# One projection per tensor with its three bf16 parts split off in PSUM, and row scatters spread two per slot over the attention slots

## The reference

```python
x = L0_attn_x                                   # (8, 512, 128)
xn = _layernorm(x, axis=-1)
x = x + attn(xn, w_attn, w_proj, decay_raw) + ffn(xn, W1, W2, Wr)

# attn: 16 heads of 8 channels, causal, with a decay over the distance
q, k, v = split(xn @ w_attn)
scores = einsum('bhqd,bhkd->bhqk', q, k) / sqrt(8) + causal + logw   # logw = -log1p(decay * log1p(dist))
y = einsum('bhqk,bhkd->bhqd', softmax(scores), v) @ w_proj

# ffn: 8 experts of 512 hidden channels, the two best of each token, weighted
gate = top-2 of softmax(xn @ Wr), renormalised
out = sum over experts of gate * (silu(xn @ W1[e].T) @ W2[e].T)
```

## Time and profile before

| | before |
|---|---|
| median of 3 runs | 726.49 us (723.21 to 731.6) |
| the profiled execution | 724.6 us, of which the trace spans 722.8 |
| PE busy | 580.9 us (80%) |
| PEld busy | 396.4 us (55%) |
| DVE busy | 340.2 us (47%) |
| ACT busy | 291.3 us (40%) |
| POOL busy | 413.9 us (57%) |

### The profile page before, as it was taken

One profiled execution on the slowest core, in us unless ns is written; L12 is line 12 of the kernel. 1 busy time (PEld: TensorE's weight loads), 2 busy tenths in 40 slices (PEclk: granted clock), 3 DMA queues, 4 the chain that ended last, 5 costly groups with the idle time before them and its releaser, 6 DMA issues.

```text
span 722.8 us, 13966 instructions
## 1 busy us (share of the span) xinstructions
PE 580.9 (80%) x4558; PEld 396.4 (55%) x4572; DVE 340.2 (47%) x1396; ACT 291.3 (40%) x521; POOL 413.9 (57%) x674
## 2 busy tenths in 40 slices
PE   0696200999999999999999999999859998899840
PEld 0275000565555555565555555665558988898840
DVE  6504800466566565475565655677213222222225
ACT  7121000565555555555555555556512222222210
POOL 1300478777686677686786776789224444344432
PEclk9999999999999999999999999999969999999985
DMA  8952011222240331322312312310715565555538
GB/s 208 181 161 88 26 52 41 67 66 71 74 125 25 124 93 50 102 71 77 101 48 75 115 34 74 104 56 16 220 41 167 171 186 173 168 178 176 174 124 274
DMA packets 76564, 79.05 MB, mean 109 GB/s; under 512 B 8766, under 2 KB 59712, under 8 KB 76496
## 3 DMA queue, kind: packets, MB, share of 16 engines
q1 hardware_dynamic: 72144, 69.70, 34.4%
q0 software_dynamic: 4352, 8.47, 3.4%
HBM read 46.49 MB, written 30.02 MB: 106 GB/s over the span
## 4 chain that ended last, share of the span: by engine, by line
PE 71%; DVE 11%; POOL 5%; issue 5%; DMA 4%; SPq 2%; ACT 1%; POOLq 0%; DVEq 0%
PE psT L1014 18%; PE psO L1026 11%; PE ps L1104 11%; PE psT L1114 9%; PE psM L967 8%; PE ps L993 6%; DVE scores L881 5%; POOL rows_dram L592 4%; PE psO L957 2%; PE psM L976 1%; DMA x_all<-x 1%; PE psM L1095 1%; PE psM L969 1%; DVE x_all L428 1%; PE ps L1059 1%
## 5 line engine op out<-in xcount | busy, mean ns | idle before, releaser
L610 POOL TENSOR_SCALAR scores<-scores,row_max 128x256 f32<-128x256 f32 (+3 forms) x512 | 264.0, 533 | 92.0 <-DVE row_max L881 89.8
L881 DVE CUSTOM_DVE_ANT_0 scores<-ps,wdist 128x256 f32<-128x256 f32 (+3 forms) x512 | 222.2, 487 | 175.3 <-PE ps L993 175.2
L676 ACT ACTIVATE probs<-psT 128x512 f32<-128x512 f32 x320 | 173.9, 595 | 137.1 <-PE psT L1014 137.1
L1014 PE MATMUL psT<-ident,scores 128*128 128x128 f32 x1280 | 175.2, 281 | 36.5 <-POOL scores L610 36.5
L1014 PEld LDWEIGHTS psT<-ident,scores 128*128 128x128 f32 x1280 | 140.5, 142 | 74.3 <-POOL scores L610 47.7
L626 POOL DMA_INDIRECT picked_dram<-values,row_ring x72 | 70.7, 982 | 98.1 <-DVE values L924 93.0
L1026 PE MATMUL psO<-probs,values 128*32 128x512 f32 (+3 forms) x1024 | 94.8, 444 | 0.0
L712 ACT ACTIVATE probs<-ps 128x512 f32<-128x512 f32 x72 | 43.0, 597 | 126.6 <-PE ps L1104 126.6
L1104 PE MATMUL ps<-values,wdist 128*128 128x128 f32 x576 | 81.0, 285 | 12.4 <-issue 11.6
L1104 PEld LDWEIGHTS ps<-values,wdist 128*128 128x128 f32 x576 | 71.4, 196 | 18.9 <-issue 18.2
L1114 PE MATMUL psT<-wdist,probs 128*128 x576 | 77.3, 278 | 0.0
(11 more groups left out here) (119 smaller groups left out, 367.9 us busy)
## 6 DMA issues: line engine op xcount, KB each, us to landing
wdist<-w1t SPq DMA_DIRECT2D x72, 256.0 KB, 3.2
k_rows<-k_dram SPq DMA_DIRECT2D x64, 96.0 KB, 2.5
q_rows<-q_dram SPq DMA_DIRECT2D x64, 96.0 KB, 2.4
rows_dram<-probs SPq DMA_DIRECT2D x1, 4680.0 KB, 34.8
row_ring<-rows_dram SPq DMA_DIRECT2D x72, 65.0 KB, 2.5
probs<-picked_dram SPq DMA_DIRECT2D x8, 512.0 KB, 7.5
k_dram<-k_parts SPq DMA_DIRECT2D x8, 384.0 KB, 2.4
q_dram<-q_parts SPq DMA_DIRECT2D x8, 384.0 KB
```

Source lines behind the costliest of these rows:

```text
L610: last = nc.gpsimd.tensor_scalar(part, part, -1.0, row_max[:, r, tile, quad:quad + 1], ALU.mult, ALU.add)
L676: nc.scalar.activation(probs[:, at.ring(2), w, :], psT[:, w % 2], ACT.Exp, scale=-1.0).then_inc(exp_ready, 1)
L881: last = nc.vector.tensor_tensor_reduce(out=scores[:, r, u, col:col + n], in0=bank[:, col:col + n], in1=wdist[:, at.g * QUADS + quad, SEQ ...
L1014: last = nc.tensor.transpose(psT[:, w % 2, place * P:(place + 1) * P], scores[:, at.ring(2), u, col + key * P:col + (key + 1) * P], ident[:])
```

## The change

1. `KB`, `KC`, `QB` and `QC` are gone. PE projects once (`KA`, `QA`) into `psM`. ACT copies the high part out (`hi_step`). DVE subtracts it in PSUM, in place (`KR`, `QR`: `rest_step`). ACT copies the middle part (`KM`, `QM`: `mid_step`), and DVE writes the rest less the middle part as the low part (`KL`, `QL`: `lo_step`), and only that frees `psM`. The bf16 minus identity is gone too.
2. The block of 32 scatters ahead of the slots is gone, and so are `send_rows`, SP's copies and their semaphores. POOL scatters two tiles per slot directly from `xn_all`, after the second `P1` step: the first picks in slots 0 to 15, the second in slots 18 to 33, with `SR` in slot 17.
3. In the prologue DVE does the four splitting steps of batch 0 between `normalise(2)` and `normalise(3)`.

```diff
-SECOND_PICK_SLOT = 3
+SENDS = 2
+SECOND_PICK_SLOT = NTILE // SENDS + 1
...
     step("P1", n, NGROUP, 1)
+    per_batch("KR", -3)
+    per_batch("QR", -2)
     step("TE", n - 1, NGROUP, 2, 4)
     step("PV", n - 2, NGROUP, 1)
-    per_batch("KB", -3)
-    per_batch("QB", -2)
+    per_batch("KM", -3)
+    per_batch("QM", -2)
     per_batch("PJ", 8)
+    if n == SECOND_PICK_SLOT:
+        steps.append(("SR", 0))
+    first = SENDS * (n if n < SECOND_PICK_SLOT else n - SECOND_PICK_SLOT - 1)
+    if 0 <= first < NTILE:
+        steps.append(("SC", first - n, int(n > SECOND_PICK_SLOT)))
     step("P1", n, NGROUP, 2)
     step("TE", n - 1, NGROUP, 4, 6)
     step("PV", n - 2, NGROUP, 2)
+    per_batch("KL", -3)
+    per_batch("QL", -2)
     step("P1", n, NGROUP, 3)
     step("TE", n - 1, NGROUP, 6, 8)
     step("PV", n - 2, NGROUP, 3)
-    per_batch("KC", -3)
     per_batch("KW", -3)
-    per_batch("QC", -2)
     per_batch("QW", -2)
...
-    step("SC", n - SECOND_PICK_SLOT - 1, NTILE)
-    if n == SECOND_PICK_SLOT:
-        steps.append(("SR", 0))
-    step("SL", n - SECOND_PICK_SLOT, NTILE)
...
-                pool.wait_ge(filled, 16)
-                pool.wait_ge(rows_ready, 1)
-                for t in range(NTILE):
-                    send_row(xn_all[:, t, :], rows_sent)
...
-                def send_step(at):
-
-                    pool.wait_ge(send_loaded[at.ring(2)], at.groups(8, 16 - 8 * at.ring(2)))
-                    nc.gpsimd.nop(nofuse=True)
-                    send_row(send_rows[at.ring(2)], second_sent[at.ring(2)])
+                def send_step(at, pick):
+
+                    if at.c == 0:
+                        if pick == 0:
+                            pool.wait_ge(filled, 16)
+                        pool.wait_ge(rows_ready, pick + 1)
+                    for t in range(at.c, at.c + SENDS):
+                        nc.gpsimd.indirect_dma_start(
+                            out=rows_dram, out_offset=bass.IndirectOffsetOnAxis(ap=xn_all[:, t, 0:1].bitcast(U32), axis=0),
+                            in_=xn_all[:, t, 1:], in_offset=None).then_inc(rows_sent, 16)
...
+                def mid_step(number, parts):
+                    def step(at):
+
+                        act.wait_ge(rest_ready, at.batches(2, number))
+                        nc.scalar.activation(parts[:, 1], psM[:], ACT.Copy).then_inc(mid_ready, 1)
+                    return step
...
+                def rest_step(number, parts):
+                    def step(at):
+
+                        dve.wait_ge(hi_ready, at.batches(2, number))
+                        nc.vector.tensor_tensor(psM[:], psM[:], parts[:, 0], ALU.subtract).then_inc(rest_ready, 1)
+                    return step
+
+                def lo_step(number, parts):
+                    def step(at):
+
+                        dve.wait_ge(mid_ready, at.batches(2, number))
+                        nc.vector.tensor_tensor(parts[:, 2], psM[:], parts[:, 1], ALU.subtract).then_inc(misc_free, 1)
+                    return step
...
                 for b in range(1, BATCH):
                     normalise(b)
+                    if b == 2:
+                        run_prologue(number_parts)
...
-                        last = mm(psM[:], w, xt[:, at.parity, :], start=True, stop=not parts)
-                        for part in parts:
-                            last = mm(psM[:], minus_ident[:], part, start=False, stop=part is parts[-1])
-                        last.then_inc(misc_full, 1)
+                        mm(psM[:], w, xt[:, at.parity, :], start=True, stop=True).then_inc(misc_full, 1)
```

More of the change, by code:

```diff
@@ L327, in build @@
             "p (r f) -> p r f", f=DFF)
-        send_rows = [sb(f"send_rows{r}", [P, TOKEN_ROW]) for r in range(2)]
         row_ring = sb("row_ring", [P, RING, ROW])
@@ L390, in build @@
         rows_sent = sem("rows_sent")
-        send_loaded = [sem(f"send_loaded{r}") for r in range(2)]
-        second_sent = [sem(f"second_sent{r}") for r in range(2)]
         slot_table = sem("slot_table")
@@ L521, in load_rows @@
                                  ).then_inc(rows_loaded[j], 16)
-                sp.wait_ge(rows_sent, 16 * NTILE)
-                for sent in second_sent:
-                    sp.wait_ge(sent, 8 * NTILE)
+                sp.wait_ge(rows_sent, 16 * TOPK * NTILE)
                 for j in range(RING):
@@ L654, in _, with hi_step @@
                         last.then_inc(wdist_ready, 1)
[L656 removed]
+                def hi_step(kind, parts, written):
                     def step(at):
                         act.wait_ge(misc_full, at.misc(kind, 1))
[L660 removed]
+                        if at.c > 0:
                             act.wait_ge(written, at.batches(48))
[L662 removed]
+                        nc.scalar.activation(parts[:, 0], psM[:], ACT.Copy).then_inc(hi_ready, 1)
+                    return step
[3 more added lines that the diff above has]
+                        nc.scalar.activation(parts[:, 1], psM[:], ACT.Copy).then_inc(mid_ready, 1)
                     return step
```

52 lines of the change are left out of this document (18 added, 34 removed).

## The result

| | before | after |
|---|---|---|
| median of the runs, us | 726.19 (723.21 to 731.6, 4 runs) | 635.25 (630.91 to 638.26, 4 runs) |
| profiled execution, us | 724.6 | 630.91 |
| its span, us | 722.8 | 629.1 |

The ratio is 0.8736 (95% interval 0.8657 to 0.8815). The forecast of 639, with 629 to 656 as its range, holds.

The account below looks back on a forecast made before the run. Bounds: a POOL stall at the start, 31 PE-bound slots, a row stall at the end. Terms -43.7 - 38.6 + 2.2 + 0.5 - 6.6 = -86.2 take 724.6 to 638.4, forecast as 639 us, range 629 to 656.

Parts of the forecast that it names:

- What bounds the kernel: Whole kernel: a POOL stall at the start, a PE-bound stretch of 31 slots, a stall for rows at the end.
- The prologue: Before attention: values' matmul starts at 33.6 instead of 41.28, 7.7 us sooner, with subtractions taken at 0.69 each.
- All up to DVE's first score step moves by 7.7: Prologue to attention's start: DVE's first score step moves from 81.11 to 73.4.
- The block of scatters: Attention's start: first TE step moves from 125.66 to 82.0, 43.7 us sooner, including the prologue's 7.7.
- The projections: Slots with keys or queries: each of 14 loses 2.76 us, 38.6 us in all.
- Cost taken: nothing: Slots with keys or queries: new subtractions are covered by DVE's free time; without cover 1.4 per slot, 20 in all.
- The scatters in the slots: Attention slots: POOL's slot becomes 10.75; PE waits add 2.2 us in early slots and 0.5 in slots 29 to 31.
- POOL as the bound: Attention slots, rival: POOL's slot passes 11.3 and bounds throughout, +20 us, 659 us in all; chance 0.06.
- the third rival: Attention slots: DVE's work holds scatters back at 3.2 each, 743 us, slower than before; chance 0.03.
- The estimate of 735: Whole kernel: time by the skill page's scatter figures, 620 ns alone and 3100 ns under a copy, about 735.
- The tail: Attention to experts: first expert matmul starts at 525.9 instead of 532.54, 6.6 us sooner.
- last rival: First slots: PE's clock stays low for two slots more, costing 8 each, 655 us; chance 0.04.

Follow-up runs that it names:

- only-split: Changed kernel with its projections kept but the earlier scatters restored (block of 32, then one per slot from send_rows): 685.05 us, ratio 0.9552.
- only-scatter: Changed kernel with its new scatter order kept but the three projections and minus_ident matmuls restored: 673.96 us, ratio 0.9378.
- select-late: Changed kernel with POOL's four causal mask selections held until DVE has normalised batch 2: 635.25 us, ratio 0.8849.
- doubled subtractions: Changed kernel with each of DVE's 32 splitting subtractions done twice, the copy into a spare tile: 647.96 us, ratio 0.9031.
- padded kernels: Changed kernel with one or three 128x256 memsets on POOL ahead of each pair of scatters: 639.4 us with one, 655.87 us with three.
- the copies on DVE: Changed kernel with four 128x512 float32 SBUF-to-SBUF copies on DVE per slot, in the third and fourth score steps: 669.61 us in one run.
- Filled waits: Changed kernel plus transposes in PE's prologue waits: 631.99 us; with splitting ahead of normalise(1) and first picks from slot 1 too: 622.78 us.

## Why the prediction was right, and where it was off

**What bounds the kernel: right.** A stall of POOL, a stretch bound by PE, a stall for rows. The only-split kernel keeps the first stall whole; the only-scatter kernel loses it and the tail's while its slots stay. The gains of the halves against 726.2, 41.1 and 52.2, come to 93.3; together they gave 90.9. Of the executions without an early rise alone (728.2 before, 685.3, 678.9, and 637.9 for both) it is 42.9 and 49.3 against 90.3. So the halves add up, to within 2 to 3 us.

**The prologue: size too large by 1.5, price right.** The subtractions took 0.69 to 0.70, as taken from the earlier trace rows. The values' matmul came at 35.09, not 33.6. The term that was off is "needs 8.54 for 28 tiles, 0.305 each, so batches 1 and 2 are done at 26.6". A mean over 28 tiles was used for the first eight; they took 3.42 us, 0.43 each, because POOL's selections run just then, and that is 1.0 of the miss. The select-late kernel shows that cause. The rest is the input, which came 0.64 later (the key projection at 22.80 instead of 22.16). The trace of the kernel before had the price to be read: its tiles by duration (shortest, median, longest, in ns), the four beside POOL's selections, then 17 behind them:

```profile
L764 DVE TENSOR_SCALAR xn_all<-x_all,mean,rstd x4: 637/668/669, 24.2 to 25.9; 128x128 f32<-128x128 f32 x4
```

```profile
L764 DVE TENSOR_SCALAR xn_all<-x_all,mean,rstd x17: 328/331/336, 26.7 to 30.8; 128x128 f32<-128x128 f32 x17
```

**"All up to DVE's first score step moves by 7.7": too small, by PE's clock.** It moved by 12.4, to 68.67. The values' matmul moved by 6.2; the other 6.2 are the router stage. The windows of this stage, in the kernel before and in the changed one:

```profile
44.00:62.00 18.00, 18.00 (x89) 18.00 (x88) 0.00 (x0) 4.18 (x7) 0.00 (x0) 1.00 0.39 128
```

```profile
38.60:45.30 6.70, 6.70 (x65) 6.70 (x65) 1.56 (x7) 2.97 (x6) 0.00 (x0) 1.00 0.77 261
45.40:82.90 37.50, 17.39 (x74) 10.80 (x74) 26.45 (x103) 5.97 (x10) 12.88 (x23) 0.50 0.19 61
```

From 44.0 to 62.15 it was 18.15 us, from 37.81 to 49.72 it is 11.9, with the same work. The clock column's 1.00 in the first row is not to be believed, for nothing had been recorded yet; the durations are (1.10 for four transposes, against 0.63 at the high clock). In the changed kernel the clock was high only for these 6.8 us: it fell at 45.4, while PE was busy without a gap, and stayed low until 82.9. Whether the change had any part in the rise can't be said from these runs (last section); a forecast by the clock of the profiled execution could not have it, and what it took off the time is luck. The profiled execution is 7.5 below the forecast's 638.4, mostly by this, and the median 4 below its 639, by the two executions with the rise: the two without, 637.53 and 638.26, are within 1.5. Without these 6.2 the traces differ by 87.5 (forecast 86.2), and the executions without an early rise by about 90 (median 728.2 of 13 before, 723.87 to 730.14).

**The block of scatters: right.** 8.6 from DVE's first score step to the `TE` step was forecast; measured 8.64. To the tenth that is luck: the forecast's terms add up to 81.8, and it wrote 81.9 and rounded up to 82.0.

**The projections: right to the hundredth.** A slot with keys or queries lost 2.76 (slot 5 from 13.96 to 11.21, slot 6 from 14.00 to 11.24). PE's timeline in one such slot has one projection now, where the earlier trace rows showed three:

```profile
210.58 1.13 PE L977 MATMUL psM<-xt,w_qkv 128*128 128x512 f32 x2 [0.35 <-DVE y L908]
211.54 1.04 PE L1021 MATMUL psT<-ident,scores 128*128 128x128 f32 x8
```

The 0.35 ahead of it is no cost of the split, for the kernel before had it at the same place:

```profile
185.84 1.13 PE L967 MATMUL psM<-xt,w_q 128*128 128x512 f32 x2 [0.35 <-DVE y L898]
```

"Cost taken: nothing" held, but with less behind it than "DVE has 40% of its time free" says: an estimated 0.87 us per slot, by the doubled subtractions.

**The scatters in the slots: right.** Slots 1 to 3 at 10.66 to 10.67 (forecast 10.75), the ten slots 113.41 (forecast 113.4), slot 30 +0.44 (forecast +0.5 for the last three), POOL at 90% (forecast 90 to 95). In all the scatters cost the slots 2.56 (forecast 2.7). POOL as the bound did not happen, and the padded kernels put its threshold between 10.93 and 11.67, round the rival's 11.3. Nor did the third rival: the copies on DVE moved the price of a scatter by 10 ns. (The estimate of 735 from the page's 3100 ns should by the forecast's own working be 737.)

**The tail: right,** 7.02 against 6.6.

**The start's clock (last rival): no.** The first `TE` step was 1.97, that of slot 2 already 1.09; the waits of slots 1 to 3 did not hold it down. What it names does occur, though: in the kernel with four scatters per slot, where PE stands idle for longer, the clock fell in attention.

## What to carry to other kernels

When one engine sends a block of work ahead of a pipeline that needs it, spread the block into the slots at a rate that keeps that engine's slot below the slot of the engine that sets the pace; measure both slots, for the busy share does not tell: POOL at 89.7% cost 2.56 us in 31 slots, and at 92.4% it set the pace. Moving an operation to an engine with free time is free up to a number that the busy share does not tell: double the operation and read the slot. A mean over a group is no price for its first members, if another engine works on the same memory just then: ask the trace for the durations of those members alone.

## What the runs showed of the hardware

**PE's clock rises early in the prologue in some executions and not in others, and that is worth 6 to 12 us.** Executions of one kernel differ by it. The mean granted clock of an execution beside its time: changed kernel 0.951 with 630.91, 0.947 with 632.97, 0.978 with 638.26, 0.982 with 637.53; only-split 0.919 with 674.83 and 0.974 to 0.976 with 683.75 to 685.75; only-scatter 0.953 and 671.1 or 669.12 against 0.985 and 676.82 or 0.982 and 681.01; and the kernel before 0.917 to 0.929 with 711.5 to 721.84 (8 of 21) and 0.972 to 0.978 with 723.87 to 730.14. By medians that is 6 us in the changed kernel, 9 in only-scatter, 10 in only-split and 12 in the kernel before. The lower mean goes with the shorter time, since the record reads 1.00 until its first change, and behind an early rise it shows the fall: the clock is low again from 45.4 to 82.9 in the changed kernel, and from 45.1 to 116.8 in only-split, through POOL's block. The profiled execution of the kernel before stays at 1.2 GHz through 18 us in which PE is busy without a gap, with matmuls of 8 columns between transposes; in the changed kernel it rose at about 38.5 in the same stage. Filled waits made the rise come in all eight executions of the two kernels that have them; why it comes at one time and not at another stays open. A comparison of two single executions would put this on the change.

**DVE and POOL get in each other's way on SBUF, DVE the more in these runs.** Beside POOL's selections of 629 ns each DVE tile takes 637 to 669 ns, one tile to one selection, and 328 to 336 without them; a copy that takes 412 to 417 ns within a scatter takes up to 2.39 us beside a row of POOL's subtractions. POOL's subtractions of 128x256 take 510 against 474 ns beside the copies, those of 128x384 581 against 580. The issue of a scatter is hardly touched (999 against 989).

**A DVE operation from PSUM into PSUM costs what the same into SBUF costs:** 694 ns for 128x512, against 686 (to bf16) and 692 (to float32). The forecast had to bound this between nothing and the double.
